# A gated delta recurrence on one core: the score products of a step moved on TensorE, and its waits thinned out

## What is computed

```python
def _step(Sst, inputs):
    q_t, k_t, v_t, a_t, b_t = inputs
    ...
    Sk = jnp.einsum('bhde,bhe->bhd', Sst, k_t)
    delta_gated = v_t - a_t[:, :, None] * Sk
    update = b * jnp.einsum('bhd,bhe->bhde', delta_gated, k_t)
    Sst = a * Sst + update
    o_t = jnp.einsum('bhde,bhe->bhd', Sst, q_t)
    return (Sst, o_t)
```

## The kernel before, in words

| product | row |
|---|---|
| scores | rec_ps_scores<-rec_qk_pe,rec_kb |
| inverse | rec_ps_end<-rec_y,rec_f_t (32 columns) |
| from_state | rec_ps_chain<-rec_gqk,rec_state_t |
| a_square | rec_ps_a<-rec_a_pair,rec_a_in_t |
| f_square | rec_ps_f<-rec_tf,rec_f_t |
| solve | rec_ps_end<-rec_z,rec_inv_t (32 columns) |
| blocks | rec_ps_tg<-rec_tg,rec_a_t |
| f_fourth | rec_ps_f<-rec_yf,rec_f_t |
| into_state | rec_ps_chain<-rec_kwp,rec_u |

## Time and profile before

### The profile page before, as it was taken

The page is one execution under the profiler, slowest core; times in us unless marked ns, Lnnn a source line. Parts: engine busy times, 40 slices in busy tenths (PEclk is TensorE's granted clock), DMA queues, the critical chain, the costliest instruction groups (busy, mean ns, idle before and its releaser), DMA issues. The chain is left out here.

```text
span 3593.4 us, 192397 instructions
## 1 busy us (share of the span) xinstructions
PE 3324.9 (93%) x83236; PEld 2774.6 (77%) x83236; DVE 2771.4 (77%) x4491; ACT 1582.6 (44%) x2344; POOL 1827.1 (51%) x1707
## 2 busy tenths in 40 slices
PE   7999997899999999995999999999996987999999
PEld 5888885676767676774999999999996765888887
DVE  6767675787878787874888888888887866676765
ACT  4454543577777777670111111111112432545454
POOL 1232322465565665654777777777775430323232
PEclk9999998899999999997999999999997998999999
DMA  3121213132323232226666667666664773212121
GB/s 117 70 105 70 105 70 130 51 95 73 105 77 97 84 97 84 86 73 153 187 186 188 187 187 187 188 187 187 189 187 143 223 229 128 105 70 105 70 105 59
DMA packets 486526, 452.84 MB, mean 126 GB/s; under 512 B 55489, under 2 KB 448833, under 8 KB 467265
## 3 DMA queue, kind: packets, MB, share of 16 engines
q1 hardware_dynamic: 484160, 449.56, 41.2%
q10 hardware_dynamic: 2304, 2.49, 0.3%
HBM read 331.33 MB, written 120.60 MB: 126 GB/s over the span
## 5 line engine op out<-in xcount | busy, mean ns | idle before, releaser
L350 POOL TENSOR_TENSOR ffn_out<-ffn_gate,ffn_xres 128x512 f32<-128x512 f32 x128 | 179.7, 1431 | 783.2 <-DVE ffn_gate L254 782.8
L784 DVE SCALAR_TENSOR_TENSOR ain_conv<-ain_padded,ain_taps,ain_conv 128x512 f32<-128x512 f32 x384 | 416.4, 1084 | 13.8 <-DVE ain_tail L781 0.3
L1444 ACT ACTIVATE rec_yf<-rec_ps_f 128x256 f32<-128x256 f32 x128 | 49.1, 384 | 636.3 <-DVE rec_f_t L1353 636.3
L885 POOL TENSOR_TENSOR ain_conv<-ain_conv,ain_term 128x512 f32<-128x512 f32 x192 | 272.1, 1417 | 16.0
L1225 POOL TENSOR_TENSOR rec_d_norm<-rec_dmat,rec_early 128x512 f32<-128x512 f32 x128 | 162.8, 1272 | 197.9 <-DVE rec_dmat L1303 197.9
L46 PE MATMUL ffn_ring<-ffn_mixkh,ffn_wkh 128*128 128x512 f32 x512 | 218.3, 426 | 6.5 <-DVE ffn_mixkl L196 6.5
L46 PE MATMUL ffn_ring<-ffn_mixrh,ffn_wrh 128*128 128x512 f32 x512 | 215.3, 420 | 9.2 <-DVE ffn_mixrl L306 9.2
L940 ACT ACTIVATE ain_buf<-ain_conv 128x512 f32<-128x512 f32 x192 | 120.9, 630 | 232.8 <-POOL ain_conv L885 147.1
L1500 PE MATMUL rec_ps_scores<-rec_qk_pe,rec_kb 32*32 32x64 f32 x8192 | 143.6, 218 | 74.2 <-issue 45.6
L46 PE MATMUL ffn_ring<-ffn_mixkh,ffn_wkl 128*128 128x512 f32 x512 | 202.8, 396 | 0.0
L46 PE MATMUL ffn_ring<-ffn_mixrh,ffn_wrl 128*128 128x512 f32 x512 | 201.7, 394 | 0.0
(11 more groups left out here) (249 smaller groups left out, 10274.4 us busy)
## 6 DMA issues: line engine op xcount, KB each, us to landing
rec_early<-coeffs SPq DMA_DIRECT2D x512, 128.0 KB, 3.0
streams<-ain_buf SPq DMA_DIRECT2D x48, 1024.0 KB, 5.1
rec_qkv<-streams SPq DMA_DIRECT2D x126, 384.0 KB, 3.3
rec_qk_pe<-streams SPq DMA_DIRECT2D x127, 256.0 KB, 3.2
rec_late<-coeffs SPq DMA_DIRECT2D x504, 64.0 KB, 2.0
ffn_xres<-in_x SPq DMA_DIRECT2D x16, 1024.0 KB
ain_x<-x SPq DMA_DIRECT2D x16, 1024.0 KB, 4.9
gate<-ain_gate SPq DMA_DIRECT2D x16, 1024.0 KB, 6.7
```

The lines of the kernel that those rows point to most:

```text
L350: added = nc.gpsimd.tensor_tensor(out[:, m, :], gate[:, m, :], xres[:, m, :], ALU.add)
L784: nc.vector.scalar_tensor_tensor(out=out[:], in0=pad[:, n:n + TOK], scalar=taps[:, u // KT, u % KT, n:n + 1], in1=out[:], op0=ALU.mult, op ...
L885: nc.gpsimd.tensor_tensor(out[:], out[:], term[:], ALU.add).then_inc(pool_conv, 1)
L1444: nc.scalar.activation(yf[:, 1], ps_f[:, :, 1, :], ACT.Copy).then_inc(f2_ready, 1)
```

## The change

On TensorE alone:

- scores(n+2), which stood first in slot n, is replaced by scores(n+3), which stands after solve(n). The slots before the loop do scores(2) too, between f_square(0) and blocks(1).
- The wait for qk_loaded, which scores(m) had, stands ahead of the matmuls of solve(n) in the loop, for step n+3; scores(m) keeps it for m below 3.
- Eleven waits of the loop's body are taken out: pt_ready (scores), g_ready (a_square), a2t_ready and tf_ready (blocks), y1_ready and y2_ready (f_fourth), f4t_ready and u_ready (inverse), state_t_ready (from_state), inv_ready (solve), kwp_ready (into_state).
- The loop has STEPS - 3 turns instead of STEPS - 2, and three slots are written out behind it.

```diff
--- before.py
+++ after.py
@@ -1491,8 +1491,6 @@
         def _(pe):
             def per_head(out, lhs_t, rhs, done, firsts=(0,)):
 
-
-
                 pe.sem_inc(pe_turns, 1)
                 for g in range(G):
                     for h in range(HG):
@@ -1502,27 +1500,24 @@
                 last.then_inc(done, 1)
 
             def scores(m):
-                pe.wait_ge(qk_loaded, 16 * (m + 1))
+
+
                 pe.wait_ge(kb_ready, m + 1)
-                if not isinstance(m, int) or m > 0:
-                    pe.wait_ge(pt_ready, m)
+                if isinstance(m, int) and m < 3:
+                    pe.wait_ge(qk_loaded, 16 * (m + 1))
                 per_head(lambda r, g: ps_scores[r, g, :, :], lambda r, g: kb[r, g, :],
                          lambda r, g: qk_pe[r, g // KT, :, g % KT, :], scores_done)
 
             def a_square(m):
 
                 pe.wait_ge(aint_ready, m + 1)
-                if not isinstance(m, int) or m > 0:
-                    pe.wait_ge(g_ready, m)
                 per_head(lambda r, g: ps_a[r, g, :, :], lambda r, g: a_in_t[r, g, :], lambda r, g: a_pair[r, :, g, :], a_squared)
 
             def blocks(m):
 
-                pe.wait_ge(a2t_ready, m + 1)
+
                 pe.wait_ge(t2_ready, m + 1)
                 pe.wait_ge(g_ready, m + 1)
-                if not isinstance(m, int) or m > 0:
-                    pe.wait_ge(tf_ready, m)
                 per_head(lambda r, g: ps_tg[r, g, :, :], lambda r, g: a2_t[r, g, :], lambda r, g: tg[r, :, g, :], tg_done)
 
             def f_square(m):
@@ -1534,49 +1529,52 @@
 
             def f_fourth(m):
 
-                pe.wait_ge(y1_ready, m + 1)
+
                 pe.wait_ge(f2_ready, m + 1)
-                if not isinstance(m, int) or m > 0:
-                    pe.wait_ge(y2_ready, m)
                 per_head(lambda r, g: ps_f2[r, g, :, :], lambda r, g: f2_t[r, g, :], lambda r, g: yf[r, :, g, :], f2_squared)
 
             def inverse(n):
-                pe.wait_ge(f4t_ready, n + 1)
+
                 pe.wait_ge(y2_ready, n + 1)
-                pe.wait_ge(u_ready, n)
                 per_head(lambda r, g: ps_end[r, g, 0, :], lambda r, g: f4_t[r, g, :], lambda r, g: y2[r, g, :], f4_done)
 
             def from_state(n):
-                pe.wait_ge(state_t_ready, n + 1)
+
                 pe.wait_ge(gqk_ready, n + 1)
+                if isinstance(n, int) and n == 0:
+                    pe.wait_ge(state_t_ready, 1)
                 pe.wait_ge(state_ready, n)
                 per_head(lambda r, g: ps_chain[r, g, 1:3, :], lambda r, g: state_t[r, g, :], lambda r, g: gqk[r, :, g, :],
                          read_done, firsts=(0, KT))
 
             def solve(n):
+
                 pe.wait_ge(z_ready, n + 1)
-                pe.wait_ge(inv_ready, n + 1)
+                if not isinstance(n, int) or n + 3 < STEPS:
+                    pe.wait_ge(qk_loaded, 16 * (n + 4))
                 per_head(lambda r, g: ps_end[r, g, 1, :], lambda r, g: inv_t[r, g, :], lambda r, g: z[r, g, :], solved)
 
             def into_state(n):
+
                 pe.wait_ge(u_ready, n + 1)
-                pe.wait_ge(kwp_ready, n + 1)
                 per_head(lambda r, g: ps_chain[r, g, 0:2, :], lambda r, g: u[r, g, :], lambda r, g: kwp[r, :, g, :], wrote,
                          firsts=())
 
             scores(0)
             a_square(0)
+            pe.wait_ge(pt_ready, 1)
             scores(1)
             blocks(0)
             a_square(1)
             f_square(0)
+            pe.wait_ge(pt_ready, 2)
+            scores(2)
             blocks(1)
             f_fourth(0)
+            pe.wait_ge(state_t_ready, 1)
 
             def slot(n):
                 more = (lambda ahead: not isinstance(n, int) or n + ahead < STEPS)
-                if more(2):
-                    scores(n + 2)
                 inverse(n)
                 from_state(n)
                 if more(2):
@@ -1584,16 +1582,18 @@
                 if more(1):
                     f_square(n + 1)
                 solve(n)
+                if more(3):
+                    scores(n + 3)
                 if more(2):
                     blocks(n + 2)
                 if more(1):
                     f_fourth(n + 1)
                 into_state(n)
 
-            with pe.Fori(0, STEPS - 2) as n:
+            with pe.Fori(0, STEPS - 3) as n:
                 slot(n)
-            slot(STEPS - 2)
-            slot(STEPS - 1)
+            for n in range(STEPS - 3, STEPS):
+                slot(n)
 
 
 def attn_out_phase(nc, tag, o_all, parts, gate_dram, src, dst, wo_dram, vec_dram):
```

## The result

| | before | after |
|---|---|---|
| median, us (lowest, highest) | 3599.26 (3595.34, 3601.95) | 3672.36 (3664.3, 3673.82) |
| profiled execution, us | 3595.39 | 3670.96 |
| its span in the profile | 3593.4 | 3669.0 |
| TensorE busy | 3324.9 (93%) | 3340.4 (91%) |
| VectorE busy | 2771.4 (77%) | 2762.6 (75%) |

The changed kernel takes 1.0199 times as long, 95% interval [1.0181, 1.0218], from four runs of each: 73 us slower. The forecast was 3660, the range 3612 to 3684.

What follows compares the result with a forecast made beforehand. TensorE, busy 93% of the span, was taken as the bound, with two loops of nearly the same length in the recurrence. Steps of 8.92 add 0.52 x 122 = 64 us to 3595.4: 3659, median about 3660, range 3612 to 3684.

Steps and rivals of the forecast that it cites:

- TensorE's half from the write to a_square: Each step, from the state write to a_square: five terms sum to 3.31 us instead of 4.05, 0.74 won.
- From a_square to the next write: Rest of the step on TensorE, now holding the scores: 5.11 us instead of 4.32, 0.79 lost.
- VectorE's turn: VectorE's loop branch, until then covered by the wait for scores: +0.44 us every fourth step, 0.11 a step.
- The load ahead of solve: Solve waits for qk_loaded: 0.76 us late every second step, 0.82 in the turn's step; four steps take 35.7.
- The eleven waits ... I cost them at nothing: Waits removed from TensorE's loop: no gain, as TensorE doesn't decide there or a product's 0.89 us covers them.
- At the start ... nothing, at most 2 us either way: Before the loop, scores(2) moves ahead of blocks(1) and out of the first step: no cost, at most 2 us.
- the three steps at the end: Last three steps of the recurrence, without scores: left out of the sum, so given no cost.
- The 122 steps of the sum: The 128 steps less three at the start and three at the end, each 0.52 us longer: 64 us.
- the load in time: Rival: the qk_pe load lands before solve needs it; step 8.53, +16 us, 3614; chance 0.15.
- Faster, TensorE's order sets the pace: Rival: TensorE's own product order decides the step, 7.87 us; 65 us less, 3533; chance 0.05.
- The clock falls: Rival: TensorE idles some 1 us a step and its granted clock drops; 40 us more, 3700; chance 0.05.
- No change: Rival: turns covered and loads in time, or compiler-added register instructions take back the waits' gain; 3597; chance 0.04.

Runs made afterwards that it cites:

- the load first: The changed kernel with SP issuing load_qk(n+4) ahead of load_early instead of load_qk(n+3) behind it: 3616.27 us, ratio 1.0058.

## Why the prediction was right, point by point

- **TensorE's half from the write to a_square**, 3.31 forecast, 3.31 measured. The five terms of the sum are in the timeline as forecast: 1.66, 0.34, 0.72, 0.45 and 0.14.
- **From a_square to the next write**, 5.11 forecast without the load. With the load first it is 8.40 less 3.31, 5.09.
- **VectorE's turn**, 0.44 forecast as bare, 0.42 measured, and half of it gone with half the turns.
- **The load ahead of solve**, four steps of 35.7 forecast; the mean steps of the four phases, the turn's step last, are 9.18, 8.49, 9.12 and 8.88, 35.67. That the sum is so near is in part luck: the forecast makes the turn's own step late by 0.82, while in the trace it is as a rule punctual and its two neighbours are late (0.85 and 0.80 in the medians). The forecast also has one lateness for every late step; in the trace landings of 2.7 to 4.1 spread it, and steps of 8.5 to 10.0 stand between those of 8.40. The chain that was named, d_norm to SP's load_early to the load, is shown by the one run that moved the load ahead of it: 51 us, against the 46 that separate 3660 from the rival's 3614.
- **"The eleven waits ... I cost them at nothing"** gave the right sum for a reason that does not hold by itself. Behind a late load they do cost nothing (1.0207 against 1.0199). Without it they cost 22 us in the moved order (3638.64 less 3616.27) and 38 in the old (3594.54 less 3556.8). That the term came out at nothing is luck: another term, the late load, hid it. The text had the price, 0.1 where a product does not cover the instruction, and had even read it between scores and inverse. It overlooked how little is covered: two instructions behind a 64-column product and one behind a 32-column product. It also overlooked that an instruction behind a wait that ends last is not covered at all (a_square, 0.09).
- **"At the start ... nothing, at most 2 us either way"**, and the three steps at the end, which the sum leaves out, are what failed. The 122 steps of the sum came out, 64 us forecast and 62.9 measured in 123. The second write is 2.3 us later against the first scores, a little over the bound. Ahead of it stands one product of scores more than before, and inverse(0) waited 1.51 for state_t; which of the two it is was not tested. The last three steps cost 5.0, where the third slot is written out behind the loop. With the 5.1 behind the recurrence, which are spread, these are the 12 us by which the median lies above 3660.
- **The rivals**: the load in time would have given 3614, and the kernel with the load first took 3616. *Faster, TensorE's order sets the pace*: a_square did wait for a_in_t. *The clock falls*: 1.00 in the steady stretch. *No change*: the ratio's interval begins at 1.0181.

## What to carry to other kernels

A product moved off one engine's critical stretch buys only what the next chain leaves: here 0.74 in one half for 0.77 in the other. It also took away two covers, one over VectorE's turn and one over the time in which a load lands, and no row of its own shows that it gave them. Test such a cover with a small delay at the place: if the time does not move there is slack, if it moves by the delay the chain is bare. And split a change that does two things: the half that was thought worthless here is the one that is worth 1%.

## What was not expected of the hardware

- Two slots of 1152 matmuls and weight loads in TensorE's loop instead of one: 1.44 times the kernel's time, with 680 instruction packets in 2600 us, where one slot has none in 1000 us. VectorE's loop went from four to eight slots without harm.
- On TensorE a register instruction ahead of a product takes 0.1 from start to start though its own duration is 32 to 36 ns. Behind a product of 64 columns two such instructions are hidden (0.89) and a third costs 0.10 (scores to inverse, 0.99); behind one of 32 columns one is hidden (0.63) and a second costs 0.08 to 0.12 (0.71 and 0.75).
- Code that TensorE runs once, outside its loop, has breaks in mid-product too: seven in the last three slots of the changed kernel, 0.57 to 2.29 us each, and from each to the next there are 127 matmuls.
- On VectorE it matters which instruction carries the wait that ends last: carried by the operation itself, it starts 0.09 sooner than behind a semaphore instruction, and 0.19 sooner than behind a register and a semaphore instruction.
